# Self-attention and feature stage of a decoder layer in one pipeline, first norm on POOL

## The chip, the cores and the metric

The kernel runs on one core of a Trainium2 chip. The metric is the device time of one execution in microseconds (us). The five engines are PE (matrix products), DVE (vector), ACT (activations and copies), POOL (GpSimd) and SP (here the issuer of most DMAs). They run their own instruction streams and meet in semaphores.

## What is computed

A pre-norm decoder layer on x of 32 sequences x 128 tokens x 128 features, with 16 heads of 8. The parts that matter here, cut from the reference:

```python
x = x + attn(layernorm(x))       # q, k l2-normalised per head; sim = q k^T / n**sigmoid(m); no softmax
x = x + xattn(ctx, ctx, layernorm(x))
x = x + ffn(layernorm(x))        # router, top 1 of 16 experts, and a shared gated MLP
# xattn: feature map of 16 numbers per head, on v, k and q alike
z = einsum('nshd,ed->nshe', x, fm_w) + fm_b
f = concatenate([exp(z), exp(-z)], axis=-1)
attn = softmax(einsum('nqhd,nkhd->nhqk', q, k) / sqrt(128)); out = attn @ v @ fc_w.T + fc_b
```

ctx has 77 keys for each sequence. Since self-attention has no softmax, it is computed as q (k^T v), with k^T v, the head mask and Wo folded into one 128x128 matrix for each sequence.

## The kernel before

Sequences go in groups of `JP` = 4, so there are `NG` = 8 groups, and a 128x512 tile holds one group. There are four stages, each with a function for each engine; semaphores order them and nothing else.

**Stage 1, self-attention** (`dve_phase1`, `act_phase1`, `pool_phase1`, `pe_phase1`). `loop1` runs a software pipeline of eleven steps with four groups in flight: `first` (statistics and norm of group t+3), `front` (transposes of the norm, products with the q, k, v weights, bias on DVE), `middle` (squares on ACT, sums, root and reciprocal on DVE, scaling of q and k by POOL, k^T v on PE, mask and scale `mt` on DVE, product with Wo, copy `mw` on ACT) and `back` (yp = q times mw, added to `xs`; statistics; second norm by ACT into `xn2`; transposed into `xT`). The root of a deviation is ACT's Sqrt and DVE's reciprocal. `wait_on_copy` puts a tiny DVE copy after some waits. PE runs five matrix products in each step whose result nothing reads (`keep_streaming`, L389). POOL adds the output bias to `xs` (L381). The middle steps are a hardware loop.

**Stage 2, features** (`*_phase2`, `loop2`). For each group PE transposes ctx, multiplies ctx and xT with the feature map, and transposes the key features into values. ACT takes exponentials: each half of key and query features once as fp32 (`kf`; `qf`, which lies in `qkv`) and once as bf16 (`kpart`, `qpart`, part 0). DVE (queries) and POOL (keys) make two more bf16 parts out of the residuals. SP sends all parts to DRAM (`qparts`, `kparts`) and reloads groups 0 and 1 for attention as `qst`, `kst`. PE starts this stage when all of `xT` is there.

**Stage 3, cross-attention** (`*_phase3`), 32 sequences: scores, maxima on DVE, scores with the shift, exponentials on ACT (L874), products with the values. POOL reloads groups 2 to 7 once all parts have been sent. **Stage 4** is the router, the shared MLP and the expert tiles.

Of the kernel before, what the change touches and what calls it, by code (L numbers as in the profile page):

```python
# [29 lines left out]
def decoder_layer(nc, t, out):  # L30
    B, S, D = t["x"].shape
    KEYS = t["ctx_1024"].shape[1]
# [24 lines left out]
    with ExitStack() as ctx:  # L57
# [3 lines left out]
        def arena(name, size):  # L61
# [4 lines left out]
            def phase():  # L66
                at = [start]
# [51 lines left out]
        carrier = sb("carrier", [P, 1])  # L119
# [13 lines left out]
        for n in ("const_in", "weights_in", "filled", "scale_in", "map_ready", "esc", "esc_dve",  # L133
# [3 lines left out]
                  "qres", "qmid", "qlo", "ctxTp", "ctxT", "zkp", "kf", "khi", "kres", "kmid", "klo", "vp", "v_ready",  # L137
                  "ap", "amax", "mhi", "mres", "mmid", "mlo", "mTp", "mT", "bp", "expd", "avp", "avs",
                  "ones_rows", "ones_in", "set", "tavp", "rden", "avn", "t2p", "t2", "fcp", "x2", "stat3", "mean3",
                  "xb2", "std3", "xn3", "h_kept", "hTp", "hT", "lgp", "rstd3", "lg", "r_step", "oh", "rankp",  # L140
# [3 lines left out]
        x_in = [sem(f"x_in{i}") for i in range(2)]  # L144
# [53 lines left out]
        def act_phase0(a):  # L198
            a.wait_ge(s["scale_in"], 16)
# [12 lines left out]
        ctx_s = [sb(f"ctx{i}", [KEYS, JP, D]) for i in range(2)]  # L212
        early = arena("early", 32768)
# [9 lines left out]
        ss = sb1("ss", [P, JP * 2 * HEADS])  # L223
        nrm = sb1("nrm", [P, JP * 2 * HEADS])
# [5 lines left out]

        def sp_phase1(sp):
            with sp.Fori(1, NG // 2) as g2:
                for par in range(2):

                    sp.wait_ge(x_in[par], g2 * 16)
                    sp.dma_start(seqs(xs, g2 * 2 + par), x_seq(g2 * 2 + par)).then_inc(x_in[par], 16)

        def loop1(eng, step, after_first=None):


            def group(g2, k):

                if isinstance(g2, int):
                    g = g2 * 2 + k
                    return (g, g % 2, g // 2) if 0 <= g < NG else None
                return (g2 * 2 + k, k % 2, g2 + k // 2)

            def at(g2, k):
                step(group(g2, k + 3), group(g2, k + 2), group(g2, k + 1), group(g2, k))
            for i in range(-3, 0):  # L250
                at(0, i)
                if i == -3 and after_first is not None:
                    after_first(eng)
# [1236 lines left out]
```

## Time and profile before

| | us |
|---|---|
| median of 3 runs | 497.67 |
| lowest, highest | 497.08, 499.48 |
| the profiled execution | 495.24 |
| its span in the trace | 493.4 |
| span of stage 1 | 0 to 117.51 |
| span of stage 2, to the last query residual | 117.51 to 181.43 |
| first exponential of attention | 192.97 |

Mean granted clock of PE: 0.961. Over the span PE is busy 84%, DVE 60%, ACT 54%, POOL 41%. In a time line a row is a run of like instructions: start, length, engine, line, operation, output and inputs, how many, and in brackets the idle time before it and what ended it. Records of one engine overlap slightly, so a start is often earlier than the last one's end. Busy time says which engine could be the limit; the brackets say which engine was waited for.

### The profile page before, as it was taken

The page shows a single profiled execution, that of the slowest core. Times are in us where ns is not written, and L with a number is a line of the kernel's source. Part 1 is how long each engine was busy: PE and PEld are TensorE (multiplying, and loading weights), DVE is VectorE, ACT ScalarE, POOL GpSimd, SP SyncE. Part 2 cuts the span into 40 slices and gives each one's busy share as a digit, 9 for nine tenths or more (in the row PEclk, how much of TensorE's full clock was granted, in tenths as well). Part 3 has the DMA queues.
Part 4 walks back from the last instruction along what each step waited for, and adds up shares of the span by engine and source line. Part 5 has one row for each costly group of instructions (what it writes and reads, how often), then busy time and mean ns, then how long its engine had stood idle before and what let it go on. Part 6 is the DMA issues. An engine that isn't in the chain of part 4 may idle for free.

```text
span 493.4 us, 10895 instructions
## 1 busy us (share of the span) xinstructions
PE 412.9 (84%) x3796; PEld 309.3 (63%) x3797; DVE 298.1 (60%) x881; ACT 264.1 (54%) x602; POOL 201.1 (41%) x280
## 2 busy tenths in 40 slices
PE   1788888876767738898999999999999997988995
PEld 1466666653444327788888888776656666677663
DVE  4787776541666665778787877365773333444446
ACT  5455555435878533777777777755563222333320
POOL 1322222111787554454555300000047753766740
PEclk9999999987998877999999999999999998999999
DMA  6940000000499994675766300000005115887729
GB/s 197 307 120 1 0 0 0 2 0 14 145 261 272 286 306 130 179 197 155 199 165 185 86 7 5 4 3 0 1 25 181 55 54 135 244 248 236 232 59 314
DMA packets 46449, 61.81 MB, mean 125 GB/s; under 512 B 7268, under 2 KB 42372, under 8 KB 44788
## 3 DMA queue, kind: packets, MB, share of 16 engines
q1 hardware_dynamic: 34800, 37.63, 25.7%
q0 software_dynamic: 4832, 20.37, 14.7%
q10 hardware_dynamic: 6768, 3.18, 2.6%
q8 instruction: 29, 0.48, 0.4%
q14 instruction: 20, 0.16, 0.1%
HBM read 43.34 MB, written 20.59 MB: 130 GB/s over the span
## 4 chain that ended last, share of the span: by engine, by line
PE 57%; DVE 18%; ACT 10%; issue 7%; SPq 3%; DMA 3%; ACTq 1%; DVEq 0%; POOL 0%
PE bank L709 6%; PE bank L698 5%; PE bank L1323 4%; PE bank L1268 3%; PE bank L1278 3%; PE bank L1277 3%; PE bank L671 3%; DVE mx L783 3%; ACT t_hT L1205 2%; PE bank L410 2%; PE bank L1324 2%; PE bank L733 2%; DMA kparts<-kpart 2%; PE bank L434 2%; PE bank L397 2%
## 5 line engine op out<-in xcount | busy, mean ns | idle before, releaser
L874 ACT ACTIVATE prob<-bank 77x512 f32<-77x512 f32 x128 | 74.4, 596 | 21.3 <-PE bank L698 21.1
L783 DVE TENSOR_REDUCE mx<-bank 128x5 f32<-128x385 f32 (+1 forms) x96 | 54.9, 576 | 17.1 <-PE bank L671 14.2
L1249 POOL DMA_INDIRECT sorted_in<-h_rows,pos_s x32 | 31.6, 986 | 80.4 <-ACT h_rows L1182 71.9
L1254 POOL DMA_INDIRECT routed<-t_y,t_no x47 | 45.4, 967 | 27.8 <-DVE t_y L1122 19.0
L698 PE MATMUL bank<-qst,kst 99*77 99x128 bf16 x512 | 50.2, 221 | 0.2 <-ACT prob L874 0.2
L377 POOL TENSOR_TENSOR qkv<-qkv,rn 128x256 f32<-128x256 f32 x32 | 19.1, 631 | 63.4 <-DVE rn L296 63.4
L1178 ACT ACTIVATE s_g<-bank 128x512 f32<-128x512 f32 x32 | 19.1, 598 | 47.3 <-PE bank L1278 33.7
L698 PEld LDWEIGHTS bank<-qst,kst 99*77 99x77 bf16 x512 | 38.5, 116 | 7.4 <-ACT prob L874 4.1
L671 PE MATMUL bank<-kst,qst 96*128 96x77 bf16 x512 | 35.6, 206 | 7.7 <-DVE mx L783 4.1
L1032 DVE TENSOR_TENSOR act<-bank,s_g 128x512 f32<-128x512 f32 x24 | 16.5, 688 | 34.9 <-ACT s_g L1178 34.9
L633 POOL DMA_DIRECT2D qst<-qparts x36 | 18.2, 505 | 47.3 <-DMA kst<-kparts 33.7
L709 PE MATMUL bank<-prob,vals 77*17 77x128 f32 x1024 | 34.2, 274 | 0.0
L1205 ACT COPY t_hT<-bank 128x128 f32<-128x128 f32 x47 | 12.5, 266 | 39.5 <-PE bank L1314 36.0
L1268 PEld LDWEIGHTS bank<-sd,act 128*128 128x128 f32 x192 | 24.8, 192 | 13.1 <-issue 9.9
L671 PEld LDWEIGHTS bank<-kst,qst 96*128 96x128 bf16 x512 | 26.9, 101 | 9.6 <-DVE mx L783 6.0
L329 ACT ACTIVATE xn<-xs,ln_bias,ln_rstd 128x128 f32<-128x128 f32 (+1 forms) x64 | 26.4, 482 | 11.4 <-DVE ln_bias L278 11.4
L567 DVE TENSOR_TENSOR res_q<-qkv,qpart 128x512 f32<-128x512 f32 x16 | 14.0, 878 | 30.5 <-ACT qpart L542 30.5
L1115 DVE TENSOR_TENSOR t_act<-bank,t_sg 128x128 f32<-128x128 f32 x47 | 13.7, 292 | 30.8 <-ACT t_sg L1209 30.7
L410 PE MATMUL bank<-first_pack,xnT 128*128 128x384 f32 x64 | 24.4, 528 | 6.8 <-ACT xnT L340 6.8
L389 PE MATMUL bank<-first_pack 128*128 128x384 f32 x80 | 29.0, 494 | 0.0
L1323 PE MATMUL bank<-t_hT,t_w 128*128 128x128 f32 x94 | 22.9, 326 | 7.0 <-ACT t_hT L1205 2.1
L709 PEld LDWEIGHTS bank<-prob,vals 77*17 77x17 f32 x1024 | 25.2, 97 | 2.8
(169 smaller groups left out, 1018.6 us busy)
## 6 DMA issues: line engine op xcount, KB each, us to landing
qst<-qparts POOLq DMA_DIRECT2D x36, 256.0 KB, 3.5
t_w<-in_expert_w SPq DMA_DIRECT2D x47, 192.0 KB, 2.5
qparts<-qpart SPq DMA_DIRECT2D x16, 384.0 KB, 7.7
kst<-kparts POOLq DMA_DIRECT2D x36, 154.0 KB, 3.9
kparts<-kpart SPq DMA_DIRECT2D x16, 231.0 KB, 7.5
sorted_in<-in_fill SPq DMA_DIRECT2D x1, 3102.0 KB, 13.4
t_row<-sorted_in ACTq DMA_DIRECT2D x47, 66.0 KB, 1.9
qst<-qparts SPq DMA_DIRECT2D x12, 256.0 KB, 6.7
```

The costliest lines, as they stand in the source:

```text
L329: i = a.activation(dst[:, j], x_of(g, j), ACT.Identity, scale=ln_rstd[k][:, j:j + 1], bias=ln_bias[k][:, j:j + 1])
L389: pe.matmul(bank[0][:, 0:3 * D], ident[:], wqkv[:], start=True, stop=True)
L410: pe.matmul(bank[1 + j][:, 0:3 * D], xnT[par][:, j * P:(j + 1) * P], wqkv[:], start=True, stop=True).then_inc(s["qkvp"], 1)
L671: i = pe.matmul(bank[n % 2][:, (h - h0) * KEYS:(h - h0 + 1) * KEYS], qst[r][0:ROWS, h, c * S:(c + 1) * S], kst[r][0:ROWS, h, c * KEYS:(c + ...
L698: i = pe.matmul(bank[2 + n % 2][0:KEYS, c * S:(c + 1) * S], kst[r][0:SHIFT_ROWS, h, t * KEYS:(t + 1) * KEYS], qst[r][0:SHIFT_ROWS, h, t * ...
L709: i = pe.matmul(bank[AV_BANK[b % 2]][32 * c:32 * c + EX + 1, u * P:(u + 1) * P], vals[:, b, 4 * u + c], prob[n % PROBS][:, c], start=True, ...
L783: v.tensor_reduce(mx[:, b % JA, h0:h1], bank[n % 2][:, 0:(h1 - h0) * KEYS].rearrange("p (h k) -> p h k", k=KEYS), AX.X, ALU.max, negate=Tr ...
L874: a.activation(prob[n % PROBS][:].rearrange("p c t -> p (c t)"), bank[2 + n % 2][0:KEYS], ACT.Exp, scale=SCORE_SCALE).then_inc(s["expd"], 1)
L1249: p.indirect_dma_start(out=sorted_in, out_offset=bass.IndirectOffsetOnAxis(ap=pos[:, b:b + 1].bitcast(U32), axis=0), in_=h_rows[:, b], in_ ...
L1254: p.indirect_dma_start(out=routed, out_offset=bass.IndirectOffsetOnAxis(ap=t_no[r][:].bitcast(U32), axis=0), in_=t_y[r][:], in_offset=None ...
L1268: i = pe.matmul(bank[BK_DOWN[par]][:, j * D:(j + 1) * D], act[c][:, j * P:(j + 1) * P], sd[:, c], start=(c == 0 and j == 0), stop=(c == CH ...
L1323: pe.matmul(bank[2 + r % 2][:, 0:P], t_w[r][:, 0:FF], t_hT[r % 2][:], start=True, stop=True)
```

## The change

Stages 1 and 2 become one pipeline of twelve steps, unrolled, in which a step handles up to five groups: `first` (t+3), `front` (t+2, now with the key features and values of that group), `middle` (t+1), `back` (t) and `last` (t-1, the query features). Beside that:

- The first norm is made by POOL with four tensor_scalar (subtract the mean, multiply by the inverse deviation), not by ACT. The second stays on ACT.
- Every inverse root is Ln and then Exp with scale -0.5 on ACT, with the reciprocals on DVE gone, in stage 3 too. One table set is loaded ahead.
- The tiny carrier copies and the products of `keep_streaming` go.
- ctx comes transposed from the host's layout, so PE's transposes and ACT's copy of it go.
- Values: one half of the copy is ACT's, one DVE's. `kf` and `qf` have one buffer instead of two. `qpart`, `kf` and `qf` lie in the memory of stage 3's `prob`, so ACT waits for all parts to be sent ahead of the exponentials.
- SP issues all x loads, the first two of ctx, the fill of `sorted_in` and the late weights at once, then the sends and reloads step by step.

The diff, cut to its core:

```diff
-        def pool_phase1(p):
-            def step(first, front, middle, back):
-                if middle:
-                    g, par, _ = middle
-                    p.wait_ge(s["rn1"], g + 1)
-                    for j in range(JP):
-                        qk = qkv[par][:, j, 0:2 * D].rearrange("p (h d) -> p h d", d=HD)
...
-            def keep_streaming(n):
-                for _ in range(n):
-                    pe.matmul(bank[0][:, 0:3 * D], ident[:], wqkv[:], start=True, stop=True)
...
+            for t in range(-3, NG + 1):
+                step(group(t + 3), group(t + 2), group(t + 1), group(t), group(t - 1))
...
+            for g in range(2, NG):
+                sp.dma_start(seqs(xs, g), x_seq(g)).then_inc(x_in[g], 16)
+            sp_fill(sp)
...
+            def step(first, front, middle, back, last):
+                k, q = front, last
+                if k is not None and k < NG - 2:
+                    sp.wait_ge(s["zkp"], k * 2 + 2)
+                    ctx_load(k + 2)
...
+                if q is not None and 1 <= q < 7:
+                    group, i = (q - 1) // 3, (q - 1) % 3 * 2
+                    if i == 0:
+                        sent(group)
+                    load(sp, group, i)
+                    load(sp, group, i + 1)
...
+            def step(first, front, middle, back, last):
+                if middle is not None:
...
+                    v.tensor_reduce(rn[:], sq[:].rearrange("p j (h d) -> p (j h) d", d=HD), AX.X, ALU.add).then_inc(s["ss1"], 1)
+                    v.wait_ge(s["ss1"], g + 1)
+                    v.tensor_scalar(rn[:], rn[:], L2_EPS * L2_EPS, None, ALU.max).then_inc(s["nmax1"], 1)
+                if first is not None:
+                    v.wait_ge(x_in[first], 16)
+                    if first > 0:
+                        v.wait_ge(s["xn1"], first)
+                    statistics(first, 0, "stat1", "mean1")
...
+                    g = back
...
+                    v.tensor_tensor(x_g, bank[7][:], x_g, ALU.add).then_inc(s["x1"], 1)
+                    v.wait_ge(s["x1"], g + 1)
+                    statistics(g, 1, "stat2", "mean2")
+                if middle is not None:
+                    g = middle
+                    v.wait_ge(s["kvp"], g + 1)
...
+                if last is not None:
+                    g = last
...
+                    for hf in range(2):
+                        v.wait_ge(s["qhi"], g * 2 + (hf + 1))
+                        v.tensor_tensor(res_q[hf][:], qf[hf], qpart[g % 2][hf][:, 0], ALU.subtract).then_inc(s["qres"], 1)
+                if front is not None:
+                    g = front
+                    v.wait_ge(s["vp"], g + 1)
+                    v.tensor_copy(values_of(g, 1), turned_keys(1)).then_inc(s["v_ready2"], 1)
+                if back is not None:
+                    bias(back, 1, "rstd2", "bias2")
+                if front is not None:
+                    for j in range(JP):
+                        v.wait_ge(s["qkvp"], front * JP + (j + 1))
+                        v.tensor_tensor(qkv[front % 2][:, j], bank[1 + j][:, 0:3 * D], bqkv[:], ALU.add).then_inc(s["qkv1"], 1)
...
+                    for hf in range(2):
+                        v.wait_ge(s["qres"], g * 2 + (hf + 1))
+                        v.tensor_copy(qpart[g % 2][hf][:, 1], res_q[hf][:]).then_inc(s["qmid"], 1)
+                    for hf in range(2):
+                        v.wait_ge(s["qmid"], g * 2 + (hf + 1))
+                        v.tensor_tensor(qpart[g % 2][hf][:, 2], res_q[hf][:], qpart[g % 2][hf][:, 1], ALU.subtract).then_inc(s["qlo"], 1)
...
+        def act_phase1(a):
+            def log_variance(g, k, mean, log_s):
+                a.wait_ge(s[mean], g + 1)
+                a.activation(ln_std[k][:], ln_mv[k][:, :, 1], ACT.Ln, bias=eps[:]).then_inc(s[log_s], 1)
+            def inverse_deviation(g, k, log_s, rstd_s):
+                a.wait_ge(s[log_s], g + 1)
+                a.activation(ln_rstd[k][:], ln_std[k][:], ACT.Exp, scale=-0.5).then_inc(s[rstd_s], 1)
...
+                a.activation(kf[hf], bank[1 + hf][:, 0:JK], ACT.Exp, bias=map_b[:, hf:hf + 1]).then_inc(s["kf"], 1)
...
+                a.activation(kpart[g % 2][hf][:, 0], bank[1 + hf][:, 0:JK], ACT.Exp, bias=map_b[:, hf:hf + 1]).then_inc(s["khi"], 1)
...
+                a.activation(qf[hf], bank[3 + hf][:], ACT.Exp, bias=map_b[:, hf:hf + 1])
...
+                a.activation(qpart[g % 2][hf][:, 0], bank[3 + hf][:], ACT.Exp, bias=map_b[:, hf:hf + 1]).then_inc(s["qhi"], 1)
...
+                if front is not None:
+                    a.wait_ge(s["xT1p"], front + 1)
+                    a.copy(xnT[front % 2][:], bank[0][:]).then_inc(s["xT1"], 1)
...
+                    a.wait_ge(s["nmax1"], middle + 1)
+                    a.activation(rn[:], rn[:], ACT.Ln).then_inc(s["nrm1"], 1)
...
+                    key_feature(front, 0)
...
+                    a.activation(rn[:], rn[:], ACT.Exp, scale=-0.5).then_inc(s["rn1"], 1)
+                if front is not None:
+                    key_feature(front, 1)
+                    key_high(front, 0)
+                    key_high(front, 1)
...
+                    log_variance(first, 0, "mean1", "log1")
+                if last is not None:
+                    query_feature(last, 0)
...
+                    inverse_deviation(first, 0, "log1", "rstd1")
+                if last is not None:
+                    query_feature(last, 1)
+                    query_high(last, 0)
+                    query_high(last, 1)
...
+                    log_variance(back, 1, "mean2", "log2")
...
+                    a.wait_ge(s["vp"], front + 1)
+                    a.copy(values_of(front, 0), turned_keys(0)).then_inc(s["v_ready"], 1)
+                if back is not None:
+                    inverse_deviation(back, 1, "log2", "rstd2")
...
+                    a.copy(qT[:], bank[5][:]).then_inc(s["qT1"], 1)
+                if back is not None:
+                    normalise(back, 1, "bias2", xn2[back % 2], "xn2")
...
+                    a.copy(mw[:], bank[6][:]).then_inc(s["mw1"], 1)
...
+                    a.copy(xT[:, back * GT:(back + 1) * GT], bank[7][:]).then_inc(s["xT2"], 1)
...
+                    a.wait_ge(s["qkv1"], front * JP + JP)
...
+                    a.activation(sq[:], qkv[front % 2][:, :, 0:2 * D], ACT.Square).then_inc(s["sq1"], 1)
...
+                if first is not None:
+                    g = first
+                    p.wait_ge(s["rstd1"], g + 1)
+                    for j in range(JP):
+                        i = p.tensor_scalar(xn[g % 2][:, j], x_of(g, j), ln_mv[0][:, j, 0:1], ln_rstd[0][:, j:j + 1], ALU.subtract, ALU.mult)
+                    i.then_inc(s["xn1"], 1)
+                    p.wait_ge(s["xn1"], g + 1)
...
+                    g = front
+                    pe.wait_ge(s["xn1"], g + 1)
...
+                    for j in range(JP):
+                        i = pe.transpose(bank[0][:, j * P:(j + 1) * P], xn[g % 2][:, j], ident[:])
+                    i.then_inc(s["xT1p"], 1)
...
+                    for hf in range(2):
+                        pe.matmul(bank[1 + hf][:, 0:JK], map_w[:, hf], ctxT[g % 2][:], start=True, stop=True).then_inc(s["zkp"], 1)
...
+                    g = back
+                    pe.wait_ge(s["qT1"], g + 1)
+                    pe.wait_ge(s["mw1"], g + 1)
...
+                if last is not None:
+                    g = last
+                    pe.wait_ge(s["xT2"], g + 1)
...
+                        pe.matmul(bank[3 + hf][:], map_w[:, hf], xT[:, g * GT:(g + 1) * GT], start=True, stop=True).then_inc(s["zqp"], 1)
...
+                if front is not None:
+                    g = front
+                    pe.wait_ge(s["kf"], g * 2 + 2)
+                    pe.wait_ge(s["xT1"], g + 1)
+                    if back is not None:
+                        pe.wait_ge(s["x1"], back + 1)
...
+                if middle is not None:
+                    g = middle
+                    for j in range(JP):
+                        pe.wait_ge(s["qkn1"], g * JP + (j + 1))
+                        i = pe.transpose(bank[5][:, j * P:(j + 1) * P], qkv[g % 2][:, j, 0:D], ident[:])
...
+                if front is not None:
+                    g = front
+                    for j in range(JP):
+                        if j < 2:
+                            pe.wait_ge(s["khi"], g * 2 + (j + 1))
+                        elif last is not None:
+                            pe.wait_ge(s["qhi"], last * 2 + (j - 1))
+                        pe.matmul(bank[1 + j][:, 0:3 * D], xnT[g % 2][:, j * P:(j + 1) * P], wqkv[:],
...
+                if back is not None:
+                    g = back
+                    pe.wait_ge(s["xn2"], g + 1)
...
@@ -888,6 +875,7 @@
             for g in range(AHEAD // JA - 1):
                 copy_shift(g)
+            all_sent(a, NG // 2)
             for n in range(STEPS):
                 b, u = n // 4, n % 4
                 exponentials(n)
@@ -969,13 +957,9 @@
         def deviation3(a, k):
             lo, hi = NORMED[k]
             a.wait_ge(s["mean3"], hi)
-            a.activation(std[:, lo:hi], mv[:, lo:hi, 1], ACT.Sqrt, bias=eps[:]).then_inc(s["std3"], 1)
-        def inverse_root(v, k):
-            lo, hi = NORMED[k]
-            v.wait_ge(s["std3"], k + 1)
-            v.reciprocal(rstd[:, lo:hi], std[:, lo:hi]).then_inc(s["rstd3"], 1)
-            v.wait_ge(s["rstd3"], k + 1)
+            a.activation(std[:, lo:hi], mv[:, lo:hi, 1], ACT.Ln, bias=eps[:]).then_inc(s["log3"], 1)
+            a.wait_ge(s["log3"], k + 1)
+            a.activation(rstd[:, lo:hi], std[:, lo:hi], ACT.Exp, scale=-0.5).then_inc(s["rstd3"], 1)
         def normalise3(v, g):
             for j in range(JP):
```

How it moves instructions. On DVE, from the addition to `xs` to the end of the step. Before, in the last steps of stage 1 (`ln_stats_50`, `ln_mv_52` are those of the second norm):

```order
L302 TENSOR_TENSOR xs<-bank,xs 128x512
L165 COPY carrier<-eps 128x1
L266 BN_STATS ln_stats_50<-xs 128x6 x4
L165 COPY carrier<-eps 128x1
L270 BN_AGGR ln_mv_52<-ln_stats_50 128x2 x4
L276 RECIPROCAL ln_rstd_56<-ln_std_54 128x4
L278 SCALAR_TENSOR_TENSOR ln_bias_58<-ln_mv_52,ln_rstd_56 128x4
L310 TENSOR_TENSOR qkv<-bank,first_pack 128x384 x4
L315 SCALAR_TENSOR_TENSOR mt<-bank,inv_scale,second_pack 128x512
```

And now, in a full step (`res_q` are the query residuals of the group one behind, `vals` one half of the front group's values):

```order
L347 TENSOR_TENSOR xs<-bank,xs 128x512
L318 BN_STATS ln_stats_50<-xs 128x6 x4
L322 BN_AGGR ln_mv_52<-ln_stats_50 128x2 x4
L353 SCALAR_TENSOR_TENSOR mt<-bank,inv_scale,second_pack 128x512
L363 TENSOR_TENSOR res_q_72<-qf_105,qpart_0_99 128x512
L363 TENSOR_TENSOR res_q_73<-qf_106,qpart_1_100 128x512
L367 COPY vals<-bank 77x32x16
L327 SCALAR_TENSOR_TENSOR ln_bias_58<-ln_mv_52,ln_rstd_56 128x4
L373 TENSOR_TENSOR qkv<-bank,first_pack 128x384 x4
L378 CAST qpart_0_99<-res_q_72 128x512
L378 CAST qpart_1_100<-res_q_73 128x512
L381 TENSOR_TENSOR qpart_0_99<-res_q_72,qpart_0_99 128x512
```

The bias of the second norm, which followed its statistics at once, now stands behind `mt`, the residuals and the values; the additions of qkv, which closed the step together with `mt`, now stand after them, with the casts and last residuals behind.

On POOL, the end of stage 1 and the start of stage 2 before (`res_k`, `kpart` are the key residuals and parts):

```order
L377 TENSOR_TENSOR qkv<-qkv,rn 128x256 x4
L381 TENSOR_TENSOR xs<-xs,first_pack 128x512
L377 TENSOR_TENSOR qkv<-qkv,rn 128x256 x8
L583 TENSOR_TENSOR res_k_85<-kf_0_71,kpart_0_79 128x308
L583 TENSOR_TENSOR res_k_86<-kf_1_72,kpart_1_80 128x308
L586 TENSOR_TENSOR kpart_0_79<-res_k_85,eps_p 128x308
L586 TENSOR_TENSOR kpart_1_80<-res_k_86,eps_p 128x308
```

And one full step now:

```order
L486 TENSOR_TENSOR qkv<-qkv,rn 128x256 x4
L493 TENSOR_TENSOR res_k_74<-kf_103,kpart_0_70 128x308
L493 TENSOR_TENSOR res_k_75<-kf_104,kpart_1_71 128x308
L496 TENSOR_TENSOR kpart_0_70<-res_k_74,eps_p 128x308
L496 TENSOR_TENSOR kpart_1_71<-res_k_75,eps_p 128x308
L499 TENSOR_TENSOR kpart_0_70<-res_k_74,kpart_0_70 128x308
L499 TENSOR_TENSOR kpart_1_71<-res_k_75,kpart_1_71 128x308
L504 TENSOR_SCALAR xn<-xs,ln_mv_51,ln_rstd_55 128x128 x4
L507 TENSOR_TENSOR xs<-xs,first_pack 128x512
```

The key residuals and the first norm now stand between one step's scaling of q and k and the bias addition, and in every step.

On ACT, the start, before:

```order
L200 ACT_TABLE_LOAD
L200 ACTIVATE inv_scale<-m_col 128x1
L202 ACTIVATE inv_scale<-inv_scale 128x1
L324 ACT_TABLE_LOAD
L324 ACTIVATE ln_std_53<-ln_mv_51,eps 128x4
L329 ACTIVATE xn<-xs,ln_bias_57,ln_rstd_55 128x128 x4
L340 COPY xnT_59<-bank 128x512
L324 ACTIVATE ln_std_53<-ln_mv_51,eps 128x4
```

And now:

```order
L193 ACT_TABLE_LOAD
L195 ACTIVATE inv_scale<-m_col 128x1
L197 ACTIVATE inv_scale<-inv_scale 128x1
L387 ACTIVATE ln_std_53<-ln_mv_51,eps 128x4
L391 ACTIVATE ln_rstd_55<-ln_std_53 128x4
L425 COPY xnT_59<-bank 128x512
L404 ACTIVATE kf_103<-bank,map_b 128x308
L404 ACTIVATE kf_104<-bank,map_b 128x308
```

The second table load is gone, the first norm's activations too, and the key features stand behind the copy of the transposed norm.

## Rows read from the trace of the kernel before

**Rows 1.** Windows, core 0: stretch, length, busy us by engine, granted clock, DMA share, GB/s.
```profile
63.49:75.63 12.14, 10.57 (x56) 7.41 (x55) 9.65 (x33) 7.17 (x16) 3.62 (x5) 1.00 0.00 0
138.01:145.00 6.99, 5.26 (x32) 3.68 (x30) 4.76 (x7) 5.96 (x13) 5.15 (x7) 1.00 1.01 239
117.51:181.43 63.92, 42.65 (x171) 25.63 (x171) 36.43 (x49) 45.12 (x89) 44.42 (x50) 0.85 0.84 233
```

**Rows 2.** Time line, DVE, one self-attention step: start, length, engine, line, op, idle before.
```profile
63.49 1.22 DVE L289 TENSOR_REDUCE ss<-sq 128x128 f32<-128x1024 f32 x1 [1.57 <-ACT sq L336]
...
65.28 0.16 DVE L278 SCALAR_TENSOR_TENSOR ln_bias<-ln_mv,ln_rstd 128x4 f32<-128x4 f32 x1
...
65.61 0.95 DVE L296 RECIPROCAL rn<-nrm 128x128 f32<-128x128 f32 x1
...
67.22 0.86 DVE L266 BATCH_NORM_STATS2 ln_stats<-xs 128x6 f32 x4
...
68.19 0.37 DVE L270 BATCH_NORM_AGGREGATE ln_mv<-ln_stats 128x2 f32<-128x6 f32 x4
...
69.13 1.15 DVE L278 SCALAR_TENSOR_TENSOR ln_bias<-ln_mv,ln_rstd 128x4 f32<-128x4 f32 x1
70.21 1.94 DVE L310 TENSOR_TENSOR qkv<-bank,first_pack 128x384 f32<-128x384 f32 x4
72.07 0.73 DVE L315 SCALAR_TENSOR_TENSOR mt<-bank,inv_scale,second_pack 128x512 f32<-128x512 f32 x1
```

**Rows 3.** POOL's same step, then single lines by source (ns min/median/max).
```profile
66.64 2.39 POOL L377 TENSOR_TENSOR qkv<-qkv,rn 128x256 f32<-128x256 f32 x4 [8.51 <-DVE rn L296]
69.00 1.27 POOL L381 TENSOR_TENSOR xs<-xs,first_pack 128x512 f32 x1
...
L589 POOL TENSOR_TENSOR kpart<-res_k,kpart x16: 757/1212/1286, 124.4 to 178.5; 128x308 bf16<-128x308 f32 x16
...
L912 POOL TENSOR_TENSOR xs<-xs,second_pack x32: 443/467/901, 179.4 to 277.4; 128x128 f32<-128x128 f32 x32
...
L567 DVE TENSOR_TENSOR res_q<-qkv,qpart x16: 693/842/1228, 124.4 to 177.1; 128x512 f32<-128x512 f32 x16
...
L570 DVE CAST qpart<-res_q x16: 414/986/990, 126.9 to 178.7; 128x512 bf16<-128x512 f32 x16
...
L573 DVE TENSOR_TENSOR qpart<-res_q,qpart x16: 676/679/939, 127.5 to 180.5; 128x512 bf16<-128x512 f32 x16
```

**Rows 4.** Time line, ACT: both stages and the first square.
```profile
16.42 1.06 ACT L336 ACTIVATE sq<-qkv 128x1024 f32<-128x1024 f32 x1 [2.93 <-DVE qkv L310]
...
70.42 1.65 ACT L329 ACTIVATE xn<-xs,ln_bias,ln_rstd 128x128 f32 x4 [1.53 <-DVE ln_bias L278]
...
74.05 0.59 ACT L364 COPY mw<-bank 128x512 f32<-128x512 f32 x1 [0.53 <-PE bank L434]
...
141.57 0.52 ACT L537 ACTIVATE kf<-bank,map_b 128x308 f32<-128x308 f32 x1 [1.03 <-PE bank L514]
...
143.19 0.70 ACT L537 ACTIVATE qkv<-bank,map_b 128x512 f32<-128x512 f32 x1
143.75 0.71 ACT L542 ACTIVATE qpart<-bank,map_b 128x512 bf16<-128x512 f32 x1
```

**Rows 5.** Time line, PE (one matrix product of fp32 stands as two records).
```profile
11.26 4.54 PE L410 MATMUL bank<-first_pack,xnT 128*128 128x384 f32 x8 [0.67 <-ACT xnT L340]
...
64.97 2.84 PE L410 MATMUL bank<-first_pack,xnT 128*128 128x384 f32 x8 [0.76 <-ACT xnT L340]
...
70.27 2.10 PE L389 MATMUL bank<-first_pack 128*128 128x384 f32 x6
```

**Rows 6.** Time line, where the feature stage ends and attention begins.
```profile
180.49 0.94 DVE L573 TENSOR_TENSOR qpart<-res_q,qpart 128x512 bf16<-128x512 f32 x1
...
189.19 0.71 POOL L633 DMA_DIRECT2D qst<-qparts  x1 [8.30 <-DMA qparts<-qpart]
...
192.97 0.59 ACT L874 ACTIVATE prob<-bank 77x512 f32<-77x512 f32 x1 [5.66 <-PE bank L698]
```

More of the change, by code:

```diff
@@ L143, in decoder_layer @@
             s[n] = sem(n)
-        x_in = [sem(f"x_in{i}") for i in range(2)]
+        x_in = [sem(f"x_in{g}") for g in range(NG)]
         c_in = [sem(f"c_in{i}") for i in range(2)]
@@ L211, in decoder_layer @@
         qkv = [sb(f"qkv{i}", [P, JP, 3 * D]) for i in range(2)]
-        ctx_s = [sb(f"ctx{i}", [KEYS, JP, D]) for i in range(2)]
-        early = arena("early", 32768)
+        ctxT = [sb(f"ctxT{i}", [P, -(-JK // 8) * 8])[:, 0:JK] for i in range(2)]
+        early = arena("early", 34368)
         sb1 = early()
@@ L229, in decoder_layer @@
         xn2 = [sb1(f"xn2_{i}", [P, JP, D]) for i in range(2)]
[L231 to L253, printed above, removed]
-            with eng.Fori(0, NG // 2 - 2) as g2:
-                at(g2, 0)
-                at(g2, 1)
-            for i in range(NG - 4, NG):
-                at(0, i)
@@ L368, in pool_phase1 @@
-        def pool_phase1(p):
-            def step(first, front, middle, back):
-                if middle:
-                    g, par, _ = middle
-                    p.wait_ge(s["rn1"], g + 1)
-                    for j in range(JP):
-                        qk = qkv[par][:, j, 0:2 * D].rearrange("p (h d) -> p h d", d=HD)
-                        r = rn[:, j * 2 * HEADS:(j + 1) * 2 * HEADS].rearrange("p (h o) -> p h o", o=1).broadcast_to([P, 2 * HEADS, HD])
-                        p.tensor_tensor(qk, qk, r, ALU.mult).then_inc(s["qkn1"], 1)
-                if first:
-                    g = first[0]
-                    p.wait_ge(s["xn1"], g + 1)
-                    p.tensor_tensor(seqs(xs, g), seqs(xs, g),
-                                    bo[:].rearrange("p (o f) -> p o f", o=1).broadcast_to([P, JP, D]), ALU.add).then_inc(s["xb1"], 1)
-            p.wait_ge(s["const_in"], 16)
-            loop1(p, step)
@@ L596, in decoder_layer @@
+        res_q = [sb1(f"res_q{hf}", [P, GT]) for hf in range(2)]
+        res_k = [sb1(f"res_k{hf}", [P, JK]) for hf in range(2)]
         late = arena("late", 72704)
@@ L612, in decoder_layer, with steps, group @@
         avnT = sb3("avnT", [P, 2 * P])
+        sb2 = late(KEPT)
+        qpart = [[sb2(f"qpart{par}_{hf}", [P, PARTS, GT], BF16) for hf in range(2)] for par in range(2)]
+        kf = [sb2(f"kf{hf}", [P, JK])[:] for hf in range(2)]
+        qf = [sb2(f"qf{hf}", [P, GT])[:] for hf in range(2)]
+        def steps(eng, step, after_first=None):
+            def group(g):
+                return g if 0 <= g < NG else None
+            for t in range(-3, NG + 1):
+                step(group(t + 3), group(t + 2), group(t + 1), group(t), group(t - 1))
+                if t == -3 and after_first is not None:
+                    after_first(eng)
```

489 lines of the change are left out of this document (194 added, 295 removed), and 4 rows, old and new, of the table s.

## The prediction

> **What bounds the kernel now.** I read the windows by stage first, then the time line of one step on each engine, then the groups by line. Self-attention fills the span up to 117.51 us, where the features' window begins [rows 1]. One of its steps lasts 12.14 us, from one square-sum reduction on DVE to the next, and in it no engine but PE is full: DVE 9.65, ACT 7.17, POOL 3.62, PE 10.57 us [rows 1]. PE's share is partly filler: three of the five `keep_streaming` matmuls take 2.10 us [rows 5], so all five about 3.5. The step is a chain across engines (the scores' copy, yp, the add to `xs`, statistics, root, bias, normalise, transpose). The feature stage is the 63.92 us from 117.51 to 181.43. One step of it near 140 us has DVE 4.76, ACT 5.96, POOL 5.15, PE 5.26 us of 6.99, at a DMA share of 1.01 [rows 1]. So the first stage is idle on POOL and ACT, the second on DVE and PE and full on the DMA engines. Attention scores start behind them: the last q residual ends at 181.43 and the first exponential starts at 192.97 [rows 6]. What ends there earlier ends the kernel earlier, unless the rest changes.
>
> **Floors of the new step.** A full step does one group of each stage. Added from the two windows [rows 1]:
> DVE 9.65 + 4.76 = 14.4; the reciprocal (0.95 [rows 2]), one bias, the reciprocals of the deviations and the three carrier copies go (six short ops of 0.16 or so, about 1.9 in all), half of the values' copy comes (no row of DVE has it; the two ops of DVE on bank data of like size took 0.49 and 0.73, I take 0.65, [rows 2]): 13.1 us.
> ACT 7.17 + 5.96 = 13.1; less the first norm's four activations (1.65, [rows 4]), the ctx copy and one values copy (0.5 each, as the 128x512 copy at its spacing [rows 4]), plus three small Exp (0.3 each, a guess from above by half the 0.59 of that copy): 11.4 us.
> PE 10.57 + 5.26, less 3.5 filler: 12.3, and under that, since ctx now comes transposed and its four narrow transposes go; I take 11.9 us.
> POOL 3.62 + 5.15 plus four tensor_scalar of 128x128. No row has that op on POOL. Its 128x128 addition took 0.47 and its 128x256 product 0.63 [rows 3]; I take 0.43 each, 1.7 in all, bounds 1.3 (half of the 256 product) and 2.5: 10.5 us.
> All four are near each other. DVE is the longest, so the new step is 13.1 us or more, in place of 12.1 + 8.0 (63.92 / 8).
>
> **One full step, walked.** Zero is the start of the reduction on DVE.
> DVE: reduction 1.22, max 0.25, statistics of the new group 0.86 + 0.40, x add 0.66 (below the 0.73 of `mt`), statistics again 1.3: ends at 4.75 [rows 2].
> ACT waits for the max; Ln, key exponential, Exp of rn: rn is ready at 2.6. Keys then to 3.8, queries (0.57 apart) to 6.5, the two small ones and a values half to 7.4, qT to 7.9 [rows 4].
> POOL: four products 2.65 to 5.04 [rows 3]. PE follows with k·v at 5.5. DVE has idled 0.8 and makes `mt` to 6.2 [rows 2].
> PE makes qkv, 2.84 for four [rows 5], to 8.2, then mw to 9.3.
> DVE: two q residuals at 0.84 [rows 3] to 7.9, values half to 8.6, then the bias of the second norm. That op took 0.16 alone and 1.15 where POOL's addition ran from 69.00 to 70.27; it ended with it [rows 2, 3]. In the new order POOL is in its key residuals here, so I price it 0.7 (bounds 0.16 and 1.2): 9.3. The four additions of qkv 1.94: 11.2. Two casts, 0.41 alone and 0.99 as they mostly were beside POOL: 1.9, to 13.1. Two last residuals 1.3 to 1.8: 14.4 to 14.9 [rows 2, 3].
> ACT behind it: second norm 9.45 to 11.1, mw, xT to 12.3, square 12.3 to 13.4 [rows 4]: in time for the reduction at 14.6. POOL: key residuals 5.0 to 10, first norm to 12, bias addition to 13.3: in time.
> So **a full step costs 14.6 us**, bound by DVE; bounds 13.2 (no port clash) and 17 (each op beside POOL waits for a whole one).
>
> **Ramps.** The first group's square starts at 16.42 now [rows 4]. The new front has no table load ahead of the first root, but keys and their transposes come ahead of qkv: I put the first reduction at 18.1, against about 17.5. The step after it has no back or last part: 5.5 to k·v, 2.8 for qkv, additions and square: 9.9. The next has no queries and is set by ACT's square: 11.5. Four full ones 58.4. The first without a new group 13.5 (its saved statistics only lengthen the wait for k·v). The one without a front 10. The last two (query features of groups 6 and 7, DVE 4.4 each plus a norm between) 15.4. Sum 136.8 us for the last q residual, against 181.43: **44.6 us less**.
>
> **What the other edits cost.** DMA: what took a share of 1.01 of the DMA engines in a step of 6.99 us [rows 1] is now spread over 14.6, about half, so the stage leaves the DMA limit; SP's queue keeps its order (keys, reloads, queries), and the queries it holds back behind four reloads are ready last anyway. The waits ahead of the exponentials are new on ACT (`all_sent`, since `prob` lies on `qpart`). POOL waited for the same sends before, until 189.19, 7.8 after the last residual, and the first exponential stood 11.5 after it [rows 6]; so 3.7 us cover the new wait, nothing is paid. Root by Ln and Exp: ACT's order has one table load ahead of all of it where it had two, so Ln, Exp, square and copies share one. That the change would not do what it says, with a load for each switch, is thereby out. I count no gain for the load that goes at the end of attention, since it stood in ACT's wait for DVE. The x loads, the ctx loads and the fill of `sorted_in` are now issued at once; a group of x is needed one step at a time, and what the second pack and ctx lose to the others is in the doubt of the ramps.
> The profiled run took 495.24 (span 493.4, 1.8 around it). 495.24 - 44.6 = 450.6. The median of the runs stands 2.4 above that run; I forecast for the median, **453 us**.
>
> **Two rules against this.** The bias op at 69.13 ended with POOL's op [rows 2, 3], while the statistics ran beside POOL's products at 0.86. The Trainium skill, "SBUF — State Buffer", section "Who interferes with whom", says that such a pair is an exclusive lock, held for a whole instruction. The bias row agrees. For the residuals it would give more than the 0.84 against 0.69 that I use; by it the step comes to 16 to 17 us, which is the first rival.
> PE's granted clock was 1.00 over the attention step with its filler, and 0.85 in the feature stage, which has none [rows 1]. The Trainium skill, "TensorE: Matmul & The Clock Gate", section "What's actually happening", says that the low clock is the default and activity releases it; the rows agree. By it, taking `keep_streaming` out is a risk; rivals (b) and (c) price it.
>
> **Rivals.**
> (a) POOL and DVE exclude each other fully. Ten us of POOL and about 4 us of port-bound DVE ops (max, residuals, bias, casts) then can't overlap, and both also wait for ACT: 16.8 a step. The twelve steps hold about 6.8 full ones (four, the first without a new group, and 0.6 for each of three ramps): 453 + 6.8 x 2.2 = 468 us. For it the bias row, against it the residuals. 12 in 100.
> (b) PE falls to its lower level (1.2 of 2.4 GHz) in most of the stage. Four qkv products took 4.54 us at the start against 2.84 warm [rows 5], a factor 1.6: 11.9 becomes 19 us a step. 453 + 6.8 x 4.4 = 483. Against it, PE is busy for 11.9 of 14.6 us in the walk, with no gap over 2 us, near the 10.57 of 12.14 which kept 1.00 [rows 1]: 4 in 100.
> (c) **Slower than before**: at the lower level PE's 19 us and its waits (14.6 - 11.9 = 2.7, for k·v, `mt` and the second norm) add up instead of overlapping, 21.7 a step: 453 + 6.8 x 7.1 = 501. It decides from a step of 21.3 us. 2 in 100.
> (d) The gain is given back in attention: if POOL's reloads of groups 2 and on came later against the exponentials, PE would wait at sequence 8. They start with the same signal as before, and PE waited for no load there. Price 5 to 10: 460. 4 in 100.
>
> **Numbers.** The forecast has 78 in 100 (441 to 462, by 13.2 and 15.5 us a step and 3 us of doubt in the ramps), the four rivals 22. The range reaches to (a): 439 to 470. 0.5% of 498 is 2.5 us, about what a measurement here can tell from no change. Faster 0.96, within 0.01, slower 0.03.
>
> **What would show it.** Right: the steps between two DVE reductions last 14 to 15.5 us; DVE busy over 85% of them; last q residual near 137; the first exponential about 11.5 later; granted clock near 1.00; the rest as before in length. Wrong: idle DVE ahead of the reduction (then ACT's square or the chain through xn2 is the bound), a bias op of 1.2 us, POOL over 13 us a step, or a longer attention stage.

## The result: faster, but by half of the forecast

| | median us | lowest to highest | kernel before beside it | ratio, 95% interval |
|---|---|---|---|---|
| changed kernel, first chip | 474.1 | 471.74 to 479.76 | 497.38 | 0.9507 (0.9448 to 0.9566) |
| the same, second chip | 469.3 | 467.16 to 476.44 | 496.24 | 0.9463 (0.9430 to 0.9496) |

Forecast were 453 and a range of 439 to 470. The gain is 23 us on the first chip and 27 on the second, where 44.6 were forecast. The second chip's median lies just inside the range and the first chip's outside. The profiled executions (479.76 and 476.44) are the longest of their chips and over 1.5% above the fastest, so their rows are used for how a step is built, and a sum over the whole span only with that in mind. The profile from the second chip has the same steps within 0.1 us; its first reduction starts 1.4 us earlier.

Windows of the changed kernel, core 0, columns as in [rows 1]: the step without query features, two full steps, and the tail from the last square-sum reduction to the last query residual.
```profile
33.56:50.65 17.09, 14.45 (x68) 12.14 (x69) 8.00 (x26) 8.51 (x21) 13.97 (x19) 0.70 0.15 44
64.18:80.58 16.40, 12.07 (x60) 8.89 (x60) 12.59 (x33) 10.53 (x24) 14.64 (x17) 0.90 0.45 132
80.58:95.87 15.29, 12.30 (x60) 9.14 (x60) 11.26 (x33) 10.52 (x24) 14.10 (x16) 0.88 0.55 155
126.78:157.36 30.58, 18.28 (x64) 10.03 (x62) 15.56 (x42) 14.39 (x30) 3.26 (x6) 0.67 0.44 133
```
The four full steps take 13.53, 16.40, 15.29 and 15.62 us. In the last three POOL is the busy engine, at 13.9 to 14.6 us, and not DVE; in the first it has 10.8 us of work, since the end of its norm falls into the second. The time lines of POOL, PE, ACT and DVE over one step show why.
```profile
75.35 5.62 POOL L504 TENSOR_SCALAR xn<-xs,ln_mv,ln_rstd 128x128 f32<-128x128 f32 x4
...
83.44 2.39 POOL L486 TENSOR_TENSOR qkv<-qkv,rn 128x256 f32<-128x256 f32 x4 [1.11 <-ACT rn L435]
...
90.03 6.14 POOL L504 TENSOR_SCALAR xn<-xs,ln_mv,ln_rstd 128x128 f32<-128x128 f32 x4
96.26 1.27 POOL L507 TENSOR_TENSOR xs<-xs,first_pack 128x512 f32<-128x512 f32 x1
```
```profile
81.03 0.66 PE L522 MATMUL bank<-first_pack,xn 128*128 128x128 f32 x4 [2.06 <-POOL xn L504]
...
81.72 0.58 ACT L425 COPY xnT<-bank 128x512 f32<-128x512 f32 x1 [1.17 <-PE bank L522]
...
83.06 0.30 ACT L435 ACTIVATE rn<-rn 128x128 f32<-128x128 f32 x1
...
85.11 0.69 DVE L347 TENSOR_TENSOR xs<-bank,xs 128x512 f32<-128x512 f32 x1 [1.50 <-PE bank L537]
...
89.23 0.75 DVE L353 SCALAR_TENSOR_TENSOR mt<-bank,inv_scale,second_pack 128x512 f32<-128x512 f32 x1 [2.11 <-PE bank L570]
```
Of the work that the next step needs, POOL makes the first norm last, from 75.35 to 80.97. PE's next step opens with the transposes of that norm, which wait 2.06 us for it. ACT's copy of them stands ahead of its `rn`, and `rn` is what POOL's products wait for: 1.11 us. So POOL, PE's queue and ACT's queue form a loop: 14.10 us of POOL and 1.11 of waiting are 15.2 of the step's 15.29. DVE has its idle time (1.50 and 2.11 us) ahead of results of PE and hardly any ahead of its reduction.

The step of 17.09 us has the longest of these waits. PE stands for 3.38 us ahead of the same transposes:
```profile
35.33 1.11 PE L522 MATMUL bank<-first_pack,xn 128*128 128x128 f32 x4 [3.38 <-POOL xn L504]
```
The granted clock is at its lower level from 34.2 to 44.4 us, so it falls in this wait, and PE then does most of the step's work at that level: its products on ctx take 2.26 us there and 1.20 in the step before. It falls for 3.4 us in each of the last three full steps as well.

All instructions of the first norm's line (ns least, median, most), and its last one of one step by itself beside what DVE did meanwhile:
```profile
L504 POOL TENSOR_SCALAR xn<-xs,ln_mv,ln_rstd x32: 782/800/2853, 7.5 to 109.2; 128x128 f32<-128x128 f32 x32
```
```profile
93.33 2.85 POOL L504 TENSOR_SCALAR xn<-xs,ln_mv,ln_rstd 128x128 f32<-128x128 f32 x1
...
93.65 0.74 DVE L378 CAST qpart<-res_q 128x512 bf16<-128x512 f32 x2
94.32 1.27 DVE L381 TENSOR_TENSOR qpart<-res_q,qpart 128x512 bf16<-128x512 f32 x2
95.87 1.22 DVE L334 TENSOR_REDUCE rn<-sq 128x128 f32<-128x1024 f32 x1 [0.28 <-ACT sq L474]
```
Alone the operation takes 0.80 us. Beside DVE's two casts and two last residuals (93.65 to 95.59, 1.94 us) it takes 2.85, about its own time and theirs together, while DVE's two casts run at 0.41 each, as the fastest of [rows 3]. Another 1.0 us of that norm's 6.14 is its first instruction, which took 1.75 beside DVE's query residuals. A norm took 3.37, 3.12, 3.18 and 3.11 us in the steps without query features, and 4.42, 5.62, 6.14 and 5.63 with them.

### The profile page after: what moved, and what is told of

Its sections match the earlier page's. It is cut to its first block, busy times and chain, and to the rows that moved or that the text cites. A ratio compares the mean times of both kernels' runs of the same rounds, so it can differ in the third digit from the quotient of the medians.

```text
span 477.9 us, 10392 instructions
## 1 busy us (share of the span) xinstructions
PE 396.9 (83%) x3685; PEld 303.9 (64%) x3685; DVE 277.8 (58%) x831; ACT 244.3 (51%) x577; POOL 228.0 (48%) x312
## 3 DMA queue, kind: packets, MB, share of 16 engines
q10 hardware_dynamic: 6768, 3.18, 2.8%
## 4 chain that ended last, share of the span: by engine, by line
PE 57%; DVE 13%; POOL 10%; ACT 7%; issue 5%; DMA 5%; SPq 1%; ACTq 1%; DVEq 0%; POOLq 0%
PE bank L694 7%; PE bank L683 6%; POOL xn L504 5%; PE bank L1252 3%; PE bank L1261 3%; PE bank L1262 3%; PE bank L1307 3%; PE bank L656 3%; PE bank L547 3%; DVE mx L770 3%; PE bank L718 2%; PE bank L528 2%; PE bank L537 2%; PE bank L985 2%; PE bank L1308 2%
## 5 line engine op out<-in xcount | busy, mean ns | idle before, releaser
L504 POOL TENSOR_SCALAR xn<-xs,ln_mv,ln_rstd 128x128 f32<-128x128 f32 x32 | 34.6, 1091 | 6.6 <-DMA first_pack<-in_first_pack 6.6
L694 PE MATMUL bank<-prob,vals 77*17 77x128 f32 x1024 | 34.2, 274 | 0.0
L1252 PEld LDWEIGHTS bank<-sd,act 128*128 128x128 f32 x192 | 24.8, 192 | 13.1 <-issue 9.9
L522 PE MATMUL bank<-first_pack,xn 128*128 128x128 f32 x32 | 7.0, 358 | 24.6 <-POOL xn L504 24.6
L1252 PE MATMUL bank<-sd,act 128*128 128x128 f32 x192 | 25.4, 277 | 1.4 <-DVE act L1016 1.3
L868 ACT COPY avs_s<-bank 128x512 f32<-128x512 f32 x32 | 18.7, 586 | 13.1 <-PE bank L694 13.1
```

Source lines behind the costliest of these rows:

```text
L504: i = p.tensor_scalar(xn[g % 2][:, j], x_of(g, j), ln_mv[0][:, j, 0:1], ln_rstd[0][:, j:j + 1], ALU.subtract, ALU.mult)
L694: i = pe.matmul(bank[AV_BANK[b % 2]][32 * c:32 * c + EX + 1, u * P:(u + 1) * P], vals[:, b, 4 * u + c], prob[n % PROBS][:, c], start=True, ...
L1252: i = pe.matmul(bank[BK_DOWN[par]][:, j * D:(j + 1) * D], act[c][:, j * P:(j + 1) * P], sd[:, c], start=(c == 0 and j == 0), stop=(c == CH ...
```

## The experiments

The theory after the result: the norm on POOL is 1.4 us dearer than priced by itself and another 1.3 to 3 us beside DVE, and stands where PE's next step waits for it. Its rival: PE's clock, no longer held up by filler, makes the steps long (0.70 in the step of 17.09, 0.67 in the tail).

### The first norm back on ACT

`e1_norm_act`: the pipeline as changed, with the first norm made as before.
```diff
 # DVE, ahead of the middle part
+if first is not None: bias(first, 0, "rstd1", "bias1")
 # ACT, behind query_high(last, 1)
+if first is not None: normalise(first, 0, "bias1", xn[first % 2], "xn1")
 # POOL
-p.wait_ge(s["rstd1"], g + 1)
-for j in range(JP):
-    i = p.tensor_scalar(xn[g % 2][:, j], x_of(g, j), ln_mv..., ln_rstd..., ALU.subtract, ALU.mult)
```


> One part undone: the first norm is again made by ACT's Identity with scale and bias (the bias op on DVE ahead of mt), all else of the pipeline kept. Theory N: the transposes of the norm no longer wait for POOL, full steps fall from about 15.6 to about 14, the start by 1.5 us, in all 8 to 14 us faster than the changed kernel (461 to 466). Theory C (PE's clock sets the steps): within 3 us of the changed kernel. The walk of the prediction gives ACT 13 us a step, so if ACT is the new bound, 14.5 and a gain of 5.

Measured: 455.43 us (454.68 to 456.90), ratio 0.9180 (0.9147 to 0.9213), so 13.9 less than the changed kernel on the same chip, at the upper end of theory N's 8 to 14. Windows of a full step and of the tail:
```profile
84.99:98.32 13.33, 10.61 (x62) 7.80 (x62) 12.01 (x33) 11.59 (x29) 8.75 (x11) 1.00 0.56 153
111.00:140.47 29.47, 15.82 (x62) 8.33 (x60) 15.55 (x42) 14.29 (x30) 3.26 (x6) 0.80 0.54 158
```
All four full steps are 13.33 to 13.35 us, and the granted clock in them is 1.00 with no filler at all. So PE's low clock in the changed kernel's full steps goes when its waits for POOL go. The step without query features falls from 17.03 us at a clock of 0.70 (on the same chip) to 13.02 at 0.87. The last query residual ends at 140.47 against 155.92 on that chip.

### Only the place of the norm

`e2_norm_first`: POOL makes the norm ahead of the key residuals of `front`, not behind them. The addition of the output bias moves with the norm; nothing else changes.
```diff
 # POOL, behind the products of middle
+if first is not None: <norm and output bias, the same seven lines>
 if front is not None: <key residuals>
-if first is not None: <norm and output bias>
```


> Only POOL's order within a step is changed: the first norm and the bias addition come ahead of the key residuals. Theory N, in the form that the place costs (the norm ends 3 us before the step does, beside DVE's casts): the norm takes 3.2 us a group in every step, PE's wait for it goes, full steps 14.2, 8 to 12 us faster than the changed kernel. In the form that only the length costs (POOL as a whole full): POOL's 11.5 us a step fit 15, no gain beyond 3. Theory C: within 3.

Measured: 462.20 us (461.24 to 464.06), ratio 0.9322 (0.9279 to 0.9365), 7.1 less than the changed kernel: just under the 8 to 12 of theory N's form by place, and well over the 3 of the form by length. POOL in one step:
```profile
77.63 2.39 POOL L486 TENSOR_TENSOR qkv<-qkv,rn 128x256 f32<-128x256 f32 x4 [3.56 <-ACT rn L435]
80.00 3.75 POOL L491 TENSOR_SCALAR xn<-xs,ln_mv,ln_rstd 128x128 f32<-128x128 f32 x4
```
The same 32 instructions take 27.4 us in all, not 34.6, as they mostly stand ahead of DVE's casts, and PE's wait for the norm is gone from the full steps, which are 13.9, 15.8, 13.2 and 13.9 us. Half of what e1 gives back hangs on place alone: on the earlier end and the lesser clash together, which this run doesn't part. Now the key residuals run beside DVE's casts, and the casts are slower (mean 605 against 420 ns).

### The norm in another form

`e5_norm_tt`: the norm stays on POOL in its place, as two tensor_tensor of 128x512.
```diff
-for j in range(JP):
-    i = p.tensor_scalar(xn[g % 2][:, j], x_of(g, j), ln_mv..., ln_rstd..., ALU.subtract, ALU.mult)
+p.tensor_tensor(xn[g % 2][:], seqs(xs, g), <mean, broadcast>, ALU.subtract)
+p.tensor_tensor(xn[g % 2][:], xn[g % 2][:], <inverse deviation, broadcast>, ALU.mult)
```


> The changed kernel with POOL's norm in another form, at the same place: two tensor_tensor of 128x512 (minus the mean, times the inverse deviation) in place of four tensor_scalar of 128x128 with column operands. By the 1.27 us of POOL's 128x512 addition these take 2.5 us alone against 3.1. If length alone counts, 0.6 us a step and 4 us in all are gained; if tensor_scalar is what DVE's casts hold up (4.4 to 6.1 us a group), up to 2.5 a step and 12 in all; if both forms are held up alike, 4 or less.

Measured: 467.82 us (461.29 to 469.40), ratio 0.9355 (0.9259 to 0.9451). The interval overlaps those of the changed kernel, which was not run on this chip (0.9463 and 0.9507), so the time does not decide between 4 us or less and up to 12; the trace has to. The rows of one step, POOL then DVE, and its window:
```profile
68.21 1.04 POOL L505 TENSOR_TENSOR xn<-xs,ln_mv 128x512 f32<-128x512 f32 x1
69.33 1.33 POOL L507 TENSOR_TENSOR xn<-xn,ln_rstd 128x512 f32<-128x512 f32 x1
```
```profile
69.35 1.59 DVE L378 CAST qpart<-res_q 128x512 bf16<-128x512 f32 x2
70.86 2.37 DVE L381 TENSOR_TENSOR qpart<-res_q,qpart 128x512 bf16<-128x512 f32 x2
```
```profile
58.24:73.15 14.91, 10.83 (x54) 7.53 (x53) 13.51 (x33) 10.15 (x24) 11.19 (x13) 0.93 0.49 142
```
The norm takes 2.37 us, and this time DVE is held: 3.96 us for the casts and last residuals that took 2.01 above. POOL's 14.1 become 11.2 and DVE's 11.3 become 13.5. The step of 14.91 is bound by DVE, almost the step of the forecast, for nearly its reasons. The collision costs about 2 us a step whichever engine is held.

The shorter norm tells most in the step without query features: PE waits 2.32 us for it and not 3.38, the clock stays at 1.00, and the step takes 12.29 us in place of 17.1. The norm itself is only 0.7 us shorter, so most of the 4.8 us goes with the clock. What keeps the clock up in one run and not in another is not shown: e1 and e4 (below) are one program up to there, wait 2.42 and 2.45 us, and take 13.02 us at 0.87 and 11.69 at 1.00.

### The norm on POOL in the old pipeline

`b0_before_unrolled` is the kernel before with its hardware loop written out; `b1_before_pool` is b0 with the first norm on POOL by tensor_scalar.
```diff
 # DVE
-scale_and_bias(first[0], 0, "std1", "rstd1", "bias1")
+v.wait_ge(s["std1"], first[0] + 1); v.reciprocal(ln_rstd[0][:], ln_std[0][:])
 # ACT
-normalise(g, 0, "bias1", xn[par], "xn1")
 # POOL, behind the products of middle
+for j in range(JP): i = p.tensor_scalar(xn[par][:, j], x_of(g, j), ln_mv..., ln_rstd..., ALU.subtract, ALU.mult)
```


> The kernel before with the hardware loop of its self-attention stage unrolled and nothing else: the base for the run with the norm on POOL. Both theories expect the kernel before within 2 us, steps of 12.1 us.

> One part of the change alone: the kernel before, unrolled, with the first norm made by POOL's tensor_scalar behind its scaling of q and k, all else as before. Theory N by length alone: POOL is idle for 8.5 us a step there, so the norm takes 3.2 us a group, is done 2 us ahead of its use, and the time is that of the kernel before within 3 us, or 1 to 3 us less since ACT is freed. Theory N by the clash with DVE: the norm runs beside DVE's bias op and statistics, the bias op of the second norm waits for one short instruction (0.8) and not for the 1.27 addition. If the norm costs 3 to 4 us a step wherever it is placed, 520 or more.

Measured beside a kernel before of 498.34: b0 499.90 (497.12 to 501.38), ratio 1.0038 (1.0005 to 1.0072); b1 494.63 (491.83 to 501.28), ratio 0.9947 (0.9904 to 0.9990). POOL of b1 in one step:
```profile
66.78 2.39 POOL L374 TENSOR_TENSOR qkv<-qkv,rn 128x256 f32<-128x256 f32 x4 [4.90 <-DVE rn L296]
69.16 3.12 POOL L379 TENSOR_SCALAR xn<-xs,ln_mv,ln_rstd 128x128 f32<-128x128 f32 x4
```
The same 3.12 us cost nothing there, as theory N by length had it; the steps even fall from 12.13 to 11.74 us, since ACT and DVE lose work and POOL waits 4.90 us ahead of its products anyway. Against b0, its proper base, b1 is 5.3 us shorter, more than forecast; 1.3 of it stand at the last square-sum reduction, the rest comes later and is not explained. The unheld price of 0.78 an instruction belongs to the operation, and what it does to the time belongs to where it is put.

### Filler, in all steps and in the tail

`e3_filler` gives the changed kernel products that nothing reads, seven a step, on both sides of the second norm's transposes. `e4_act_tail` is e1 with such products only in the last steps.
```diff
 # e3, back part of PE
+if front is not None: pe.wait_ge(s["v_ready"], front + 1)
+keep_streaming(3)
 pe.wait_ge(s["xn2"], g + 1)
 ...
+keep_streaming(4)
```
```diff
 # e4, against e1
+if front is None:
+    pe.wait_ge(s["v_ready"], NG)
+    keep_streaming(2 if middle is not None else 6)
 pe.wait_ge(s["xn2"], g + 1)
 ...
+if front is None: keep_streaming(1)
 # behind the last step
+keep_streaming(3)
```


> Filler products on PE put back in the pipeline: three ahead of the wait for the second norm, four behind its transposes (about 0.65 us each). Theory C: granted clock 1.00 from the second step on, the step without queries (17.1 us) falls to 13, the tail by 3 to 5, in all 6 to 12 us faster than the changed kernel. Theory N: steps unchanged at 15.3 to 15.6 in the middle, a gain in the tail of 3 us or none at all.

> The first norm on ACT, as in e1_norm_act, and filler products on PE in the last three steps alone, where PE idles and its clock fell: two ahead of the second norm's transposes in the tenth step, six in the eleventh, one behind them, three behind the last query features. Theory C for the tail (clock 0.67 to 0.80 there, query products 3.1 and 3.6 us against 1.9): they fall to 1.9 and the tail by 3 to 4 us, 451 to 453. If the clock isn't held by that, no difference beyond 1 us.

Measured: e3 473.44 (467.73 to 475.50), ratio 0.9472 (0.9410 to 0.9534), no gain on the changed kernel's 0.9463, where theory C had 6 to 12 us. e4 450.97 (450.31 to 455.84), ratio 0.9104 (0.9036 to 0.9173), the fastest kernel here, ahead of before and of the change. A full step of e3, then the tail of e4:
```profile
95.73:110.45 14.72, 14.72 (x76) 10.43 (x75) 11.66 (x32) 10.30 (x24) 13.18 (x16) 1.00 0.53 149
```
```profile
110.45:136.16 25.71, 21.46 (x90) 12.33 (x89) 15.56 (x42) 14.39 (x30) 3.26 (x6) 0.95 0.60 182
```
At a clock of 1.00 e3's full steps are 14.72, shorter than the changed kernel's 15.2 in the mean but still 1.4 over e1's, and PE is full with the filler itself, so the run can't say how much of its step is filler. It does say that in the full steps the clock alone is not what was lost. For the step without query features it is no test: its filler stands behind PE's wait for the norm (3.37 us) and not in it, the clock is low from 33.2 to 43.4 as before, and with the filler the step takes 18.97 us, not the 13 of theory C. In the tail, where each engine waits for another, the clock counts: 29.47 us at 0.80 in e1, 25.71 at 0.95 in e4, as theory C for the tail had it. The two query products (four records) behind the last group's yp show both levels, in the changed kernel and in e4:
```profile
139.08 3.62 PE L547 MATMUL bank<-xT,second_pack 128*128 128x512 f32 x4
```
```profile
121.88 1.88 PE L551 MATMUL bank<-xT,second_pack 128*128 128x512 f32 x4
```
The ratio, 1.93, is near the 2 between 2.4 and 1.2 GHz. e1 and e4 ran on different chips and their ratios' intervals overlap; the 3.8 us are a reading of the two traces.

The last run, `c0_after`, was the changed kernel beside e1 to e3, and stands in the first table.

> The changed kernel again, as the one the others are compared with on this chip. Theory N (POOL's tensor_scalar norm is long, 0.8 us alone and more beside DVE, and late) and theory C (PE's clock in gaps) both expect about 472 to 476 us, ratio 0.95, full steps of 15.3 to 16.4 us between DVE's reductions, the norm 3.1 us a group without queries beside it and 4.4 to 6.1 with them.

## Why the prediction was right or wrong

The terms of the forecast beside the same stretches of the changed kernel (first chip) and of e1 (from one square-sum reduction to the next):

| stretch, us | forecast | changed | e1 |
|---|---|---|---|
| first reduction at | 18.1 | 23.0 | 19.9 |
| step without back and last part | 9.9 | 10.6 | 12.1 |
| step without query features | 11.5 | 17.1 | 13.0 |
| four full steps | 58.4 | 60.8 | 53.4 |
| first step without a new group | 13.5 | 15.3 | 12.7 |
| tail to the last query residual | 25.4 | 30.6 | 29.5 |
| last query residual at | 136.8 | 157.4 | 140.5 |
| from there to the first exponential | 11.5 | 11.2 | 12.2 |
| rest of the span | 300.4 | 309.3 | 302.4 |

At the last query residual the changed kernel is 20.6 us over the forecast, about what its median is over (21.1). Of these the full steps hold only 2.4. The step without query features has 5.6, the start 4.9, the tail 5.2 and the step without a new group 1.8.

**What was right.** The two stages overlap as said: the last query residual moves from 181.43 to 157.36. ACT loads one table, at 0.73, and no other up to the end of attention. There is no new wait ahead of the exponentials: 11.2 us from the last residual against 11.5 [rows 6], so the wait for all parts is covered. The DMA share of the last three full steps is 0.45 to 0.55, half of [rows 1]. Rivals (b), (c) and (d) did not come as priced: PE's granted clock is 0.86 in the mean up to the last query residual, so PE is at its lower level for 28% of that time and not for most of it, and attention's exponentials take 593 ns each (594 before).

**The step that failed: the price of POOL's norm.** I had no row for a tensor_scalar on POOL and took 0.43 us, near the tensor_tensor of its size (0.47 [rows 3]), with an upper end of 2.5 us a group. It took 0.80 alone, 3.1 a group, and 4.4 to 6.1 beside DVE's casts and residuals; so POOL had 13.9 to 14.6 us in three of the four full steps and not 10.5. With it, "first norm to 12, in time" became late, and the time showed as PE's wait of 2.0 to 3.4 us for the norm, as ACT's behind it, and as the fall of the clock in the longest of these waits. The forecast named POOL over 13 us a step as a sign of being wrong, and that is what stands there. Undoing this one edit, on one chip, takes 15.5 us off the last query residual: 1.7 at the first reduction, 4.0 in the step without query features, 7.5 in the four full steps, 2.6 in the next, 1.1 in the tail, less 1.5 in the first step. It brings the time to 455.4, inside the range, though partly by errors that cancel.

**What is left with the norm on ACT** is 3.7 us at the last query residual, but as a difference of two larger errors. The full steps were forecast 5.0 us too long and the one after them 0.8: DVE does 12.0 us of work in 13.33 where I had 13.1 and 14.6, mostly by the clash below. Start and ramps were 9.6 too short: 1.8 at the start (the first qkv products take 3.45 us in e1 and 4.70 in the changed kernel, where I used the warm 2.84 although the cold 4.54 stood beside it [rows 5]), 2.2 and 1.5 in the next steps, and 4.1 in the tail. The start varies: e4, the same program up to there, has 4.15 us for these products and its first reduction 0.8 later. The profile gives a granted clock of 1.00 for the start in every trace, so that PE is slow there is read from its rows and not from the clock. e4 names the tail's: with filler in its waits it takes 25.7, where the forecast had 25.4 at warm prices. I had priced the lower clock for the whole stage (rivals (b) and (c)) and not for its thin parts, where it came: the tail (0.67, and 0.80 in e1) and, in the changed kernel, the step without query features (0.70).

**The clash of DVE and POOL** was priced on DVE's side, 0.7 for the bias op and 1.9 for two casts. The bias op takes 0.14 us and two casts 0.74, and DVE is busy 74 and 77% of the two full steps, not over 85. The wait fell on POOL. Rival (a), full exclusion at 468 us, has the right mechanism and is the nearest case to both medians, but its sum of POOL's 10 us and DVE's 4 had the cheap norm in it, and the key residuals of the changed kernel mostly ran unheld. That the second chip's 469.3 lies inside the range, which was drawn out to (a), is therefore luck. The Trainium skill, "SBUF — State Buffer", section "Who interferes with whom", says that the order of issue decides which of the two blocks, and that it blocks whole. The 2.85 us agree with the second part: POOL was held through four DVE instructions in a row. The starts in the trace don't tell the first: POOL's record begins 0.32 us before the casts and POOL is held; in e5 it begins 0.02 us before them and DVE is held.

**The rest of the span.** From the first exponential to the end it is 309.3 us where before had 300.4, 307.5 in the second chip's profile, 302.4 in e1 and 301.5 in e4. Attention is not the place: its 128 exponentials start over 130.0 us in the kernel before and over 129.4 in the changed one (132.0 on the second chip), so rival (d) is out. In the router and the tiles PE's granted clock dips at places that differ from run to run, for 3.4 us in before, 3.4 in the second chip's profile and 10.3 and 6.9 in the first's. The profiled execution is 5.7 us above its median and the second chip's 7.1, so about 3 us of the excess, or none, stand in the medians. What makes the dips is open.

## What to carry over

An operation moved to an engine that hasn't run it has no price until that operation, with its operands, is timed there; a neighbour of the same size was wrong by a factor of 1.9. Ask next which instructions of another engine hold it up at that point, and whether a result that the next step opens with is made last: the same norm cost nothing where POOL waited anyway, 7 us by its place and 14 in all here. Price the thin parts of a pipeline, its ends above all, by the nearest cold row. Filler paid in the tail; in the full steps, where PE had work enough, it did not.

## What the runs showed of the hardware

- POOL's tensor_scalar with two operands from columns, 128x128 fp32, takes 0.78 us at least; its tensor_tensor of the same size takes 0.47, and one of 128x512 1.04 with one operand broadcast. So the form with one tensor is the dearer. The Trainium skill, "GPSIMD Engine Reference", section "Engine selection", has two-input operations as the slow ones on GpSimd and one-input ones near VectorE's rate; these rows go against it, and DVE's tensor_scalar of 128x128 (with constants, L336) takes 0.23.
- DVE's small operations are held too. The limit of the norms (L336) takes 0.23 us alone, and 1.26 where POOL's addition of the output bias ran:
```profile
65.43 1.26 DVE L336 TENSOR_SCALAR rn<-rn 128x128 f32<-128x128 f32 x1
...
65.35 1.26 POOL L507 TENSOR_TENSOR xs<-xs,first_pack 128x512 f32<-128x512 f32 x1
```
